# Routed experts of a mixture ranked on the chip by their number of tiles, and their weights loaded and split by rank along the loop, four instead of seven ahead of it

## The chip, the cores and the metric

One core of a Trainium2 chip runs the whole program. The metric is the device time of one execution in microseconds. Its engines are TensorE (PE; its weight loads are PEld), VectorE (DVE), ScalarE (ACT), GpSimd (POOL), and SyncE (SP), which here only issues DMAs.

## The reference, cut to what matters

The network has two layers on 2048 tokens of width 512. The change lies in the second half of the first layer, a mixture of experts: 2 shared experts that all tokens use, and 16 routed experts of which each token uses 4.

```python
flat = u.reshape(-1, d)                                  # 2048 x 512, layer norm of x
h = jax.nn.relu(jnp.einsum('td,ndf->ntf', flat, shared_w1) + shared_b1[:, None, :])
out = flat + jnp.einsum('ntf,nfd->td', h, shared_w2) + shared_b2.sum(0)
scores = jax.nn.sigmoid(flat @ centroids.T) + bias
vals, idx = jax.lax.top_k(scores, KR)                    # KR = 4 of NR = 16 experts
gating = jnp.zeros_like(scores).at[jnp.arange(T)[:, None], idx].set(vals)
gating = gating / jnp.clip(gating.sum(-1, keepdims=True), 1e-08)
# for each expert: rout += (relu(flat @ w1 + b1) @ w2 + b2) * g[:, None];  w1 512x352, w2 352x512
x = x + jnp.tanh(g_ffn[0]) * (out + rout)
```

## The kernel before

`phase_ffn` holds three stages; the attention and the second feed-forward part of layer 2 follow in `phase_back` and are untouched.

**Shared stage.** 16 blocks of 128 tokens go through a pipeline in 24 beats (`beats`): per block a norm on DVE, the two shared experts on PE (`up`: 72 matmuls of 128 columns, `down`: 18 of 512), the routing (`route`, `choose`, `count`, `place`) and four indirect DMAs from POOL (`scatter`) that write each (token, gate) pair into its expert's list in DRAM. DVE writes the result of a block in `finish`, SP stores it in `store`; `finish` of block n waits until the store of block n-2 has landed. While this runs, SP loads the first routed experts (`early`), ACT rounds them to the high f16 part (`split`, L1124) and DVE makes the low part (`low`, L1257), each in two halves. Before, these are 7 experts (`EARLY = 7`), one in every second beat from 5 on, both halves in one beat.

**Table.** When all lists are known, DVE computes in `table` how many tiles of 128 tokens each expert has (at least one) and which expert and which list row each of the N2 = 79 tiles uses. `numbers` turns the result into a row by two small matmuls, and DVE writes it as integers to `tab2`. SP's `lists_done` waits for it and for the lists, and loads the entries of tiles 0 to 3 (L991).

**Routed loop.** 79 tiles, in the order of the experts 0 to 15, whatever their sizes. A tile: SP loads its 128 entries (`entry_load`, L991), POOL gathers 128 rows of x (`roxg`, L1070), PE transposes them (L279; the output's name alternates between ps_shpR and ps_shpC), DVE copies them to SBUF (`evacuate`, L1311), PE does 36 matmuls with w1 (`rup`, L1444), ACT the relu (`rhidden`), ACT and DVE the high and low part, PE 9 matmuls with w2 (`rdown`, L1433), ACT scales by the gate (`rout`), POOL adds the rows to DRAM (L1077). PE works in beats: transposes of tile b, `rdown` of tile b-3, `rup` of tile b-1. Only the entries of tiles 0 to 11 are loaded without a condition; from 12 on SP loads those of tile b when the gather of tile b-2 has landed (`entries`), and the gather of a tile also waits for PE's transposes two tiles before. Both engines run in their program's order, so what SP waits for in between delays later entries.

The worst case is one tile for every expert, so expert n must be ready at tile n. Experts 7 to 13 are loaded right after the shared stage, expert 14 after the split of 13, the last in eight pieces; the splits are in these beats, and PE waits by itself:

```python
late_beat = {n: beat for n, beat in zip(range(EARLY, direct), (3, 4, 5, 7, 8, 9, 10, 12))}
small_beats = (12, 13, 14, 15)
...
e.wait_ge(S.sem("rolo"), 2 * (direct - 1))      # SP, last_weights, ahead of entry loads that follow
...
pipeline(e, N2, [..., (ready, 1, 0, direct), (small_ready, 1, direct, NR), ...], unroll=8)    # PE
```

`pipeline` writes a beat out as plain code where the set of its stages changes, and makes a hardware loop of `unroll` beats where at least two such rounds have the same set. PE's loop covers tiles 18 to 73 before (7 rounds of 8). The query weights of the next phase (1024 KB) are loaded in the loop at beat 42 (`query_weights`, L1037).

Of the kernel before, what the change touches and what calls it, by code (L numbers as in the profile page):

```python
# [175 lines left out]
def build(nc, a, out):  # L176
    with ExitStack() as ctx:
# [8 lines left out]
        def dram(name, shape, dt=f32):  # L186
# [23 lines left out]
            "tab2": sb(ctx, "tab2", [1, 2, N2], i32),  # L210
# [239 lines left out]
class Front:  # L450
# [68 lines left out]
    def sync(self, e):  # L519
# [18 lines left out]
        e.dma_start(small["part"][:, :], a["c_part"]).then_inc(S.sem("sh_part"), 16)  # L538
        for n in range(KEY_FIRST):
            keys.store_values(e, n)  # L540
# [302 lines left out]
PIECES = 4  # L843

# [13 lines left out]
def phase_ffn(nc, S, sb, ps, a, R, K, shared, routed, wt_at):  # L858
# [10 lines left out]
    EARLY, FIRST = 7, 12  # L869
    direct = NR - 1  # L870
    QW, QBEAT = KD * D, 42
    with ExitStack() as mem:
# [10 lines left out]
        part = sb(mem, "shpart", [P, 1])  # L883
# [9 lines left out]
        first_slots = wt_at + (NR - EARLY - 2) * 2 * EW  # L893
        near, far = Place(nc, nc.sbuf_base, first_slots), Place(nc, first_slots, nc.sbuf_top)
        front = Front(nc, S, a, R, K, shared, {"b1r": b1r, "bias": bias, "rb1": rb1, "part": part, "vt": vt, "sq": ksq, "ss": kss, "rr": krr}, far, near, pH, pY, pR)
# [23 lines left out]
        cnt, limit, tiles, skip, past = (sb(mem, "sh" + n, [P, NR]) for n in ("cnt", "limit", "tiles", "skip", "past"))  # L919
        sums = [sb(mem, f"shsums{i}", [P, NR]) for i in range(2)]  # L920
        more = sb(mem, "shmore", [P, NR, NR])
        which = sb(mem, "shwhich", [P, 2])
        tabf = sb(mem, "shtabf", [P, 2], f16)
# [17 lines left out]

        q_at, q_raw = final(0), final(1) // 2
# [15 lines left out]
        def _(e):  # L958
# [15 lines left out]

            def weights(n):
                at = raw_at(n)
                if n == 0:
                    S.wait(e, "kyv", turn_of(NT - 1))
                if n == EARLY - 2:
                    for p in range(2):  # L980
                        S.wait_moved(e, "kykout", turn_of(NT - 1 - p))
                e.dma_start(raw[:, at:at + W1], a["rw1"][n]).then_inc(S.sem(f"roraw{n}"), 16)
                e.dma_start(raw[:, at + W1:at + W1 + W2], a["rw2"][n]).then_inc(S.sem(f"roraw{n}"), 16)
# [18 lines left out]
            def lists_done(it):  # L1002
# [3 lines left out]
                e.wait_ge(S.sem("shtable"), 2)  # L1006
                first_entries(0, 4)

# [14 lines left out]
            def last_weights(it):  # L1023
                e.wait_ge(S.sem("rolo"), 2 * (direct - 1))
                weights(direct - 1)

            def small(it):
                for i in range(2):
                    j = (it.n - small_beats[0]) * 2 + i
# [3 lines left out]
                    e.dma_start(piece[j % 2][:, 0:cols], a[src][direct][:, at:at + cols]).then_inc(S.sem(f"ropiece{j % 2}"), 16)  # L1033
# [4 lines left out]
            pipeline(e, N2, [(entries, 0, FIRST, N2), (query_weights, 0, QBEAT, QBEAT + 1), (last_weights, 2, late_beat[direct - 2], late_beat[direct - 2] + 1),  # L1038
                             (small, 2, small_beats[0], small_beats[1]), (small, 2, small_beats[1], small_beats[-1] + 1)])

        @blk.gpsimd
        def _(e):
# [19 lines left out]
            for n in range(N2 + 5):  # L1062
# [10 lines left out]
                if n >= 5:  # L1073
                    it = It((n - 5) // 2, (n - 5) % 2)
                    S.wait(e, "roy", it)
# [7 lines left out]
        def _(e):  # L1083
# [34 lines left out]
            def split(n):  # L1118
                e.wait_ge(S.sem(f"roraw{n}"), 32)
                if n >= 2:  # L1120
                    e.wait_ge(S.sem("rolo"), 2 * (n - 1))
# [1345 lines left out]
```

## Time and profile before

| what | value |
|---|---|
| time, median of 3 runs | 1187.44 us (1183.65 to 1187.78) |
| profiled execution, first to last instruction (span) | 1172.7 us |
| its own time, what lies around the span included | not recorded for it alone; the three runs lie 11.0 to 15.1 us above the span |
| busy share of the span | PE 84%, DVE 60%, ACT 57%, POOL 43% |
| TensorE's mean granted clock | 0.946 |
| bytes moved | 170.87 MB, mean 146 GB/s; the highest of 40 slices 370 GB/s |
| one expert's weights | a DMA of 704 KB and one of 768 KB |
| shared stage on PE | 243.4 to 398.0 us |
| routed loop on PE | 398.0 to about 780 us |

The busy share is a mean over stages with different limits; a stage is read by the waits of PE in it. A timeline row gives start, duration, engine, line, operation, output<-inputs and, in brackets, how long the engine was idle before it and what ended that. SPq rows are the DMA issues of SP.

### The profile page before, as it was taken

How to read it: one execution, taken by the hardware profiler on the slowest of the kernel's cores; microseconds unless marked ns; L12 is line 12 of the kernel's file. 1: busy time of each engine (PE TensorE's matmuls, PEld its weight loads, DVE VectorE, ACT ScalarE, POOL GpSimd, SP SyncE). 2: the span in 40 equal slices, each digit the busy share in tenths (PEclk: the TensorE clock that was granted, in tenths of full speed). 3: DMA queues.
4: the chain of work that ended last, by engine and by line, in shares of the span. 5: the costliest groups of instructions: out<-in, count | busy, mean ns of one | idle time of the engine just before them, and what ended most of it. 6: DMA issues, size and time to landing. Idle time of an engine off the chain costs nothing. (4 is left out here: it accounts for less than half of the span.)

```text
span 1172.7 us, 27955 instructions
## 1 busy us (share of the span) xinstructions
PE 990.9 (84%) x9515; PEld 567.5 (48%) x9516; DVE 705.2 (60%) x1724; ACT 672.1 (57%) x1091; POOL 504.0 (43%) x442
## 2 busy tenths in 40 slices
PE   5888989968999978899999999955899888888740
PEld 2545556445677656677777777742122211111120
DVE  8676755578888457322223222216688787877687
ACT  4655545445544267444445444435777789899950
POOL 0222232156676265555556555532233343433422
PEclk9999999998999989999999999987899999999975
DMA  6534231389985496766666666648598687497211
GB/s 234 178 127 138 82 129 62 130 194 229 227 209 138 132 370 155 148 122 112 120 146 117 116 117 117 119 68 219 134 178 172 154 187 145 102 180 147 65 42 64
DMA packets 183494, 170.87 MB, mean 146 GB/s; under 512 B 137173, under 2 KB 138773, under 8 KB 182485
## 3 DMA queue, kind: packets, MB, share of 16 engines
q1 hardware_dynamic: 155554, 111.62, 36.9%
q0 software_dynamic: 25888, 56.43, 24.1%
q10 hardware_dynamic: 1954, 1.54, 0.4%
q8 instruction: 60, 0.98, 0.4%
q14 instruction: 38, 0.30, 0.1%
HBM read 80.82 MB, written 65.20 MB: 125 GB/s over the span
## 5 line engine op out<-in xcount | busy, mean ns | idle before, releaser
L2020 ACT ACTIVATE sb_atp<-ps_atpS 128x1024 f32<-128x1024 f32 x256 | 242.6, 1037 | 40.5 <-PE ps_atpS L1759 40.5
L1444 PEld LDWEIGHTS ps_shpH<-sb_roxT,sb_rowt 128*128 (+1 forms) x2844 | 170.3, 107 | 20.7 <-DVE sb_roxT L1311 1.8
L1444 PE MATMUL ps_shpH<-sb_roxT,sb_rowt 128*128 128x128 f16 (+1 forms) x2844 | 174.7, 221 | 1.6 <-DVE sb_roxT L1311 1.6
L1433 PE MATMUL ps_shpY<-sb_rowt,sb_rohhl 128*128 (+1 forms) x711 | 170.4, 386 | 3.3 <-DVE sb_rowt L1324 2.9
L1771 PE MATMUL ps_atpO<-sb_atp,sb_atv 128*17 128x512 f32 x1024 | 137.3, 609 | 34.0 <-ACT sb_atp L2020 28.7
L1167 ACT ACTIVATE sb_roh<-ps_shpH,sb_rob 128x128 f32<-128x128 f32 (+1 forms) x237 | 68.8, 361 | 103.5 <-PE ps_shpH L1444 100.6
L1070 POOL DMA_INDIRECT sb_roxg<-xn,sb_roentry x79 | 85.1, 1077 | 87.9 <-DMA sb_roentry<-list 62.0
L1433 PEld LDWEIGHTS ps_shpY<-sb_rowt,sb_rohhl 128*128 128x128 f16 (+1 forms) x711 | 67.4, 99 | 71.6 <-issue 7.8
L1156 ACT ACTIVATE sb_roy<-ps_shpY,sb_roentry 128x512 f32<-128x512 f32 x79 | 54.2, 686 | 78.6 <-PE ps_shpY L1433 75.0
L1058 POOL DMA_INDIRECT list<-sb_shentry,sb_shposb x64 | 74.0, 1157 | 33.5 <-DVE sb_shposb L1239 18.5
L1077 POOL DMA_INDIRECT x2a<-sb_roy,sb_roentry x40 | 65.5, 1637 | 44.2 <-ACT sb_roy L1156 41.8
L1311 DVE COPY sb_roxT<-ps_shpR 128x1024 f16<-128x1024 f16 x40 | 27.6, 690 | 94.0 <-PE ps_shpR L279 94.0
L1077 POOL DMA_INDIRECT x<-sb_roy,sb_roentry x39 | 62.1, 1593 | 49.5 <-ACT sb_roy L1156 48.2
L1759 PE MATMUL ps_atpS<-sb_atq,sb_atk 64*128 64x512 f16 x512 | 79.9, 392 | 1.4 <-DMA sb_atq<-qst 0.6
L1311 DVE COPY sb_roxT<-ps_shpC 128x1024 f16<-128x1024 f16 x39 | 26.9, 690 | 84.7 <-PE ps_shpC L279 84.7
L1316 DVE TENSOR_TENSOR sb_rohhl<-sb_roh,sb_rohhl 128x384 f16<-128x384 f32 x79 | 44.2, 560 | 41.8 <-ACT sb_rohhl L1172 41.7
L1369 PEld LDWEIGHTS ps_shpH<-sb_shxT,sb_shw 128*128 128x128 f16 (+1 forms) x1152 | 67.5, 108 | 3.3
L1369 PE MATMUL ps_shpH<-sb_shxT,sb_shw 128*128 128x128 f16 (+1 forms) x1152 | 68.6, 222 | 0.0
L1379 PE MATMUL ps_shpY<-sb_shw,sb_shhh 128*128 128x512 f16 (+1 forms) x192 | 61.7, 405 | 7.2 <-DVE sb_shhl L1244 7.2
L1771 PEld LDWEIGHTS ps_atpO<-sb_atp,sb_atv 128*17 128x17 f32 x1024 | 17.2, 96 | 94.9 <-ACT sb_atp L2020 86.0
L820 PE MATMUL ps_shpY<-sb_ctx,sb_l1hh 128*128 (+1 forms) x152 | 46.8, 390 | 18.2 <-issue 13.8
L810 PE MATMUL ps_shpH<-sb_l1xT,sb_ctx 128*128 128x128 f16 x912 | 60.1, 223 | 0.8 <-issue 0.7
(355 smaller groups left out, 1771.5 us busy)
## 6 DMA issues: line engine op xcount, KB each, us to landing
sb_rowt<-rw SPq DMA_DIRECT2D x15, 768.0 KB, 9.6
sb_rowt<-rw SPq DMA_DIRECT2D x15, 704.0 KB, 6.5
kst<-sb_kykp SPq DMA_DIRECT2D x16, 512.0 KB, 3.5
qst<-sb_quqp SPq DMA_DIRECT2D x12, 512.0 KB, 4.0
vst<-sb_kyvt SPq DMA_DIRECT2D x16, 272.0 KB
sb_atv<-vst SPq DMA_DIRECT2D x32, 136.0 KB, 3.9
sb_stage<-ctxT SPq DMA_DIRECT2D x4, 1024.0 KB, 7.4
sb_shxin<-x SPq DMA_DIRECT2D x16, 256.0 KB, 5.4
```

Source lines behind the costliest of these rows:

```text
L810: last = e.matmul(self.pP[n % 2][:, f * P:(f + 1) * P], w[:, bass.ds(ex * W + (k * D + f * P), P)], self.xT[n % 2][:, x0 + k, :], start=j ...
L1058: S.moved(e.indirect_dma_start(out=R["list2"], out_offset=bass.IndirectOffsetOnAxis(ap=posb[it.p][:, k:k + 1], axis=0), in_=entry[:, it.n, ...
L1070: S.moved(e.indirect_dma_start(out=xg[it.p][:, :], out_offset=None, in_=R["xn2"], in_offset=bass.IndirectOffsetOnAxis(ap=rentry[:, n, 0:1] ...
L1077: S.moved(e.indirect_dma_start(out=R["x1" if it.p else "x2a"], out_offset=bass.IndirectOffsetOnAxis(ap=rentry[:, n - 5, 0:1], axis=0), in_ ...
L1167: last = e.activation(rh[0:n, f * P:(f + 1) * P], rpH[it.p][0:n, f * P:(f + 1) * P], ACT.Relu, bias=rb1[0:n, bass.ds(ex["bias"] * FB + f, ...
L1369: last = e.matmul(pH[it.p][s][0:n, f * P:(f + 1) * P], w[:, o:o + n], x[:, k, :], start=j == 0, stop=j == len(terms) - 1)
L1379: last = e.matmul(pY[it.p][:, :], x[0:n, s, k * P:(k + 1) * P], w[0:n, s * W2 + k * D:s * W2 + (k + 1) * D], start=j == 0, stop=j == len(t ...
L1433: last = e.matmul(pY[it.p][:, :], hhl[it.p][0:n, x, k * P:(k + 1) * P], weight(value, 2 * W1 + w + k * D, n, D), start=j == 0, stop=j == l ...
L1444: last = e.matmul(rpH[it.p][0:n, f * P:(f + 1) * P], weight(ex["up"], w + k * FF + f * P, P, n), rxT[it.p][:, x + k, :], start=j % (3 * KD ...
L1759: last = e.matmul(pS[n % 3][:, s * SEQ:(s + 1) * SEQ], k[at][r, j, m * P:(m + 1) * P], q[at][r, j, :], start=True, stop=True)
L1771: last = e.matmul(pO[it.p][32 * i:32 * i + n, :], vv[it.n % 3][:, m, i * n:(i + 1) * n], pr[(it.n * 8 + 2 * m + i // 2) % 6][:, (i % 2) * ...
L2020: S.done(e.activation(pr[n % 6][:, :], pS[n % 3][:, :], ACT.Exp, scale=HD ** -0.5 / SA ** 2), "atexp")
```

## The change

Experts 0 to 3 keep ranks 0 to 3. The 12 others get a rank by their number of tiles, most tiles first, computed in `table` with all-pairs comparisons. Tiles run in the order of rank; with the large ones first, rank r cannot come before tile 4 + ceil(60 (r-4)/12), so ranks 4, 5, ... 15 are needed at tiles 4, 9, 14, ... 59. SP reads the row offset of the expert of a rank from `order` into a register and loads by that address. Splits run four tiles ahead, one half in each of two beats; the early ones come every third beat. A third row of `tab2` gives the expert for the bias. PE does not wait for the splits by itself any more: DVE waits for its own (`low_done`) before it hands on a tile.

```diff
+EARLY = 4
+def needed_at(rank):
+    return rank if rank < EARLY else EARLY + -(-(NT * KR - EARLY) * (rank - EARLY) // (NR - EARLY))
...
-        early_beat = {5 + 2 * k: k for k in range(EARLY)}
-        late_beat = {n: beat for n, beat in zip(range(EARLY, direct), (3, 4, 5, 7, 8, 9, 10, 12))}
-        small_beats = (12, 13, 14, 15)
+        early_beat = {5 + 3 * k: k for k in range(EARLY)}
+        split_at = {n: needed_at(n) - 4 for n in range(EARLY + 1, direct)}
+        split_at[EARLY], split_at[direct - 2], split_at[direct - 1] = 1, 43, 49
+        load_at = {n: split_at[n] - 2 for n in range(EARLY + 3, direct - 1)}
+        load_at[direct - 1] = split_at[direct - 1] - 1
+        small_at = (51, 53, 55, 57)
+        small_load = (51, 54, 56, 58)
...
+            def expert_rows(n):
+                if n < EARLY:
+                    return slice(n * P, (n + 1) * P)
+                return bass.ds(e.value_load(K["order"][0:1, n:n + 1], min_val=0, max_val=(NR - 1) * P), P)
...
+                if n > EARLY:
+                    e.wait_ge(S.sem("rolo"), 2 * (n if n == direct - 1 else n - 1))
+                rows = expert_rows(n)
+                e.dma_start(raw[:, at:at + W1], a["rw1"][rows, :]).then_inc(S.sem(landed(n)[0]), 16)
...
-                e.wait_ge(S.sem("shtable"), 2)
+                e.wait_ge(S.sem("shtable"), 3)
                 first_entries(0, 4)
+                e.wait_ge(S.sem("shorder"), 1)
+                weights(EARLY)
+                first_entries(4, 8)
...
-            for n in range(EARLY, direct - 1):
-                weights(n)
-                first_entries(min(2 * (n - EARLY) + 4, FIRST), min(2 * (n - EARLY) + 6, FIRST))
...
+            weights(EARLY + 1)
+            first_entries(8, FIRST)
+            weights(EARLY + 2)
...
-            pipeline(e, N2, [(entries, 0, FIRST, N2), (query_weights, 0, QBEAT, QBEAT + 1), (last_weights, 2, late_beat[direct - 2], late_beat[direct - 2] + 1),
+            pipeline(e, N2, [(entries, 0, FIRST, N2), (query_weights, 0, QBEAT, QBEAT + 1)] + [late(n) for n in load_at]
+                     + [(small, 0, beat, beat + 1) for beat in small_load])
...
-            def split(n):
-                e.wait_ge(S.sem(f"roraw{n}"), 32)
+            def split(n, half):
+                if half == 0:
+                    e.wait_ge(S.sem(landed(n)[0]), landed(n)[1])
...
+                tail(v.tensor_tensor(sortkey[:, :], tiles[:, :], mul, ALU.mult))
+                tail(v.tensor_tensor(sortkey[:, :], sortkey[:, :], add, ALU.add))
+                tail(v.tensor_tensor(before[:, :, :], cols(sortkey), rows(sortkey), ALU.is_ge))
+                tail.go(v.tensor_reduce(place_[:, :], before[:, :, :], AX.X, ALU.add))
...
+                    S.done(v.tensor_reduce(K["order"][0:1, :], more[0:1, :, :], AX.X, ALU.add), "shorder")
...
-                for i in range(2):
+                for i in range(3):
                     last = e.matmul(pCw[0:1, 2 * NR + i * N2:2 * NR + (i + 1) * N2], tabf[:, i:i + 1], K["ident"][:, 0:N2], start=True, stop=True)
...
-            pipeline(e, N2, [(ahead, 0, 1, N2 + 3), (turn, 0), (ready, 1, 0, direct), (small_ready, 1, direct, NR), (both, 1, 0, N2 + 2), (rup, 1)], unroll=8)
+            e.wait_ge(S.sem("rolo"), 2 * EARLY)
+            pipeline(e, N2, [(ahead, 0, 1, N2 + 3), (turn, 0), (both, 1, 0, N2 + 2), (rup, 1)], unroll=8)
```

SP issues the store of block 13 in the same beat as `lists_done` and after it. With the changed stage list PE's loop covers tiles 4 to 75 (9 rounds of 8). `QBEAT` goes from 42 to 44. POOL waits for the last stores of the shared stage before its first addition of rows.

## Rows read from the trace of the kernel before

**Rows 1.** Windows: stretch, us, busy PE, PEld, DVE, ACT, POOL, granted clock, DMA share, GB/s.
```profile
240.00:312.00 72.00, 56.03 (x641) 39.65 (x639) 63.45 (x178) 36.66 (x74) 43.75 (x40) 0.88 0.91 212
312.00:398.00 86.00, 86.00 (x1035) 62.27 (x1033) 66.42 (x212) 39.43 (x93) 56.92 (x53) 1.00 0.65 155
496.30:767.20 270.90, 265.97 (x3180) 200.88 (x3181) 76.72 (x121) 126.66 (x301) 153.91 (x120) 1.00 0.66 120
```

**Rows 2.** Timeline, TensorE in the early shared stage.
```profile
285.85 1.03 PE L1379 MATMUL ps_shpY<-sb_shw,sb_shhh 128*128 128x512 f16 x2 [2.99 <-DVE sb_shhl L1244]
```

**Rows 3.** The two lines that split routed weights: ns min/median/max, first and last start.
```profile
L1257 DVE SCALAR_TENSOR_TENSOR sb_rowt<-sb_rowt x30: 1619/1688/1754, 256.9 to 466.0; 128x1408 f16<-128x1408 f32 x15, 128x1536 f16<-128x1536 f32 x15
...
L1124 ACT ACTIVATE sb_rowt<-sb_rowt x30: 1364/1422/1475, 253.2 to 464.3; 128x1408 f16<-128x1408 f32 x15, 128x1536 f16<-128x1536 f32 x15
```

**Rows 4.** Timeline, TensorE from tile 0's up product to tile 18.
```profile
401.55 3.76 PE L1444 MATMUL ps_shpH<-sb_roxT,sb_rowt 128*128 128x128 f16 x36 [1.59 <-DVE sb_roxT L1311]
...
407.66 0.61 PE L279 MATMUL ps_shpC<-sb_ident,sb_roxg 128*128 128x128 f16 x8
...
417.07 1.04 PE L279 MATMUL ps_shpR<-sb_ident,sb_roxg 128*128 128x128 f16 x8 [4.85 <-DMA sb_roxg<-xn,sb_roentry]
...
424.05 0.61 PE L279 MATMUL ps_shpC<-sb_ident,sb_roxg 128*128 128x128 f16 x8
...
456.94 0.61 PE L279 MATMUL ps_shpR<-sb_ident,sb_roxg 128*128 128x128 f16 x8
...
485.90 2.76 PE L1433 MATMUL ps_shpY<-sb_rowt,sb_rohhl 128*128 x9 [2.88 <-DVE sb_rowt L1324]
...
496.31 0.61 PE L279 MATMUL ps_shpR<-sb_ident,sb_roxg 128*128 128x128 f16 x8 [0.24 <-issue]
```

**Rows 5.** Timelines, SP's queue and VectorE, at the handover and at tile 13.
```profile
391.80 3.76 SPq L991 DMA_DIRECT2D sb_roentry<-list  x4
...
395.60 5.64 SPq L967 DMA_DIRECT2D x2a<-sb_shxo  x3
...
456.28 0.33 SPq L982 DMA_DIRECT2D sb_rowt<-rw  x1
...
457.98 1.56 SPq L991 DMA_DIRECT2D sb_roentry<-list  x2
...
383.79 0.42 DVE L1271 TENSOR_REDUCE sb_shtiles<-sb_shmore 128x16 f32<-128x256 f32 x1
...
399.63 0.48 DVE L1249 TENSOR_SCALAR sb_shxs<-sb_shxs,sb_gate 128x512 f32<-128x512 f32 x1 [3.82 <-DMA x2a<-sb_shxo]
```

**Rows 6.** Timelines, TensorE and POOL: loop turn, plain tile, query load, last tile.
```profile
563.32 0.61 PE L279 MATMUL ps_shpC<-sb_ident,sb_roxg 128*128 128x128 f16 x8
...
568.53 0.61 PE L279 MATMUL ps_shpR<-sb_ident,sb_roxg 128*128 128x128 f16 x8 [0.65 <-issue]
...
577.41 0.61 PE L279 MATMUL ps_shpR<-sb_ident,sb_roxg 128*128 128x128 f16 x8
...
581.81 0.61 PE L279 MATMUL ps_shpC<-sb_ident,sb_roxg 128*128 128x128 f16 x8
...
600.38 0.62 PE L279 MATMUL ps_shpC<-sb_ident,sb_roxg 128*128 128x128 f16 x8 [0.79 <-DMA sb_roxg<-xn,sb_roentry]
...
614.81 0.61 PE L279 MATMUL ps_shpR<-sb_ident,sb_roxg 128*128 128x128 f16 x8
...
767.21 0.61 PE L279 MATMUL ps_shpR<-sb_ident,sb_roxg 128*128 128x128 f16 x8
...
587.82 0.98 POOL L1070 DMA_INDIRECT sb_roxg<-xn,sb_roentry  x1 [0.67 <-DMA sb_roentry<-list]
```

**Rows 7.** Landings: gathers undisturbed, gathers under weight loads, entry loads under them.
```profile
DMA to landing us min/median/max: 3.4/4.1/4.8
...
DMA to landing us min/median/max: 3.2/6.8/8.3
...
DMA to landing us min/median/max: 4.7/7.5/10.8
```

More of the change, by code:

```diff
@@ L918, in phase_ffn @@
         gr = sb(mem, "shgr", [P, 1])
[L919 to L923, printed above, removed]
+        cnt, tiles, sortkey, place_, sums, past = (sb(mem, "sh" + n, [P, NR]) for n in ("cnt", "tiles", "sortkey", "place", "sums", "past"))
+        more, before = (sb(mem, "sh" + n, [P, NR, NR]) for n in ("more", "before"))
+        which = sb(mem, "shwhich", [P, 3])
+        tabf = sb(mem, "shtabf", [P, 3], f16)
         assert nc.sbuf_base <= first_slots
@@ L1267, in table @@
                 tail.start(It(0, 0))
+                limit, mul, add, past_last, row, place1 = (rankc[:, i, :] for i in range(6))
+                rows = lambda z: bcast(z[:, 0:1], [(1, NR), (0, NR)])
+                cols = lambda z: bcast(z[:, 0:1], [(0, NR), (1, NR)])
                 tail(v.scalar_tensor_tensor(cnt[:, :], K["iota"][:, :], -float(CAP), base[NT % 2][:, :], ALU.mult, ALU.add))
-                tail(v.tensor_scalar(limit[:, :], K["iota"][:, :], float(P), None, ALU.mult))
-                tail(v.tensor_tensor(more[:, :, :], bcast(cnt[:, 0:1], [(1, NR), (0, NR)]), bcast(limit[:, 0:1], [(0, NR), (1, NR)]), ALU.is_gt))
+                tail(v.tensor_tensor(more[:, :, :], rows(cnt), cols(limit), ALU.is_gt))
@@ new lines, in table @@
+                tail(v.tensor_tensor(sortkey[:, :], sortkey[:, :], add, ALU.add))
+                tail(v.tensor_tensor(before[:, :, :], cols(sortkey), rows(sortkey), ALU.is_ge))
+                tail.go(v.tensor_reduce(place_[:, :], before[:, :, :], AX.X, ALU.add))
+                tail(v.tensor_tensor(more[:, :, :], before[:, :, :], cols(tiles), ALU.mult))
+                tail(v.tensor_reduce(sums[:, :], more[:, :, :], AX.X, ALU.add))
+                tail(v.tensor_scalar(past[:, :], sums[:, :], part[:, 0:1], None, ALU.is_le))
@@ new lines, in table @@
+                tail.go(v.tensor_tensor(cnt[:, :], past[:, :], tiles[:, :], ALU.mult))
+                tail(v.tensor_reduce(which[:, 0:1], past[:, :], AX.X, ALU.add))
+                tail.go(v.tensor_scalar(sums[:, :], place_[:, :], 1.0, which[:, 0:1], ALU.subtract, ALU.is_equal))
+                tail(v.tensor_reduce(which[:, 1:2], cnt[:, :], AX.X, ALU.add))
+                tail.go(v.tensor_tensor(which[:, 1:2], which[:, 1:2], part[:, 1:2], ALU.subtract))
+                tail(v.tensor_tensor(sums[:, :], sums[:, :], past_last, ALU.mult))
@@ L1289, in numbers @@
+                tail(v.tensor_tensor(more[0:1, :, :], cols(place_[0:1, :]), rows(place1[0:1, :]), ALU.is_equal))
+                tail(v.tensor_tensor(more[0:1, :, :], more[0:1, :, :], cols(row[0:1, :]), ALU.mult))
+                with nc.allow_low_precision(reason="one whole number"):
+                    S.done(v.tensor_reduce(K["order"][0:1, :], more[0:1, :, :], AX.X, ALU.add), "shorder")
             def numbers(it):
                 v.wait_ge(S.sem("shrow"), 1)
-                S.done(v.tensor_copy(K["tab2"][0:1, 0, :], pCw[0:1, 2 * NR:2 * NR + N2]), "shtable")
```

138 lines of the change are left out of this document (73 added, 65 removed).

## The prediction

> **What bounds the kernel now.** I first read the windows of the stages, then TensorE's timeline for the places where it waits, then who is late there. The reader is to see three different limits [rows 1]. In the early shared stage (240 to 312 us) VectorE is busy 63.5 of 72 us and TensorE only 56.0, at a granted clock of 0.88; TensorE waits for VectorE there, as in the row with 2.99 us, one of three such waits [rows 2]. From 312 us to the end of the stage TensorE is busy for the whole 86 us, so nothing that leaves VectorE's queue there can be won. In the routed loop from tile 18 TensorE is again the limit, 266 of 271 us. A plain tile takes 4.40 us (577.41 to 581.81) [rows 6]. Between tile 0 and tile 18 it isn't: that is where the kernel loses time. Tile 3 to 4 takes 9.41 us, 4 to 5 6.98, 5 to 12 together 32.89 against 7 x 4.40 = 30.8, and 12 to 18 39.37 against 26.4, a loss of 13.0 [rows 4]. The waits behind these have names. TensorE waits 4.85 us for the gather of tile 4 and 2.88 us for a piece of the last expert, and again for a gather at tile 13. There the reason is SP: it holds the load of expert 14 back until 456.28, and the entries of the next tiles are issued behind it, at 457.98 [rows 5]. After a 4.85 us wait the eight transposes take 1.04 us instead of 0.61, so the clock has gone to its lower level, 1.2 GHz, and a part of the loss is that [rows 4].
>
> **Part A, the shared stage.** A split costs VectorE two instructions of 1.69 us and ScalarE two of 1.42 [rows 3]. Three of seven leave the stage. Of those before tile-beat 10, where VectorE limits, experts 0, 1 and 2 become experts 0 and 1: 3.4 us less on VectorE, and one half instead of two in a beat. Against it, the load of expert 1 now stands in SP's queue directly ahead of a block's input, which VectorE needs next. A wait of TensorE also costs clock, 0.88 on the mean of this stretch. The bounds are 0 (the late input eats it) and 9 us (all three waits, 2 to 3 us each, with half as much again of lower clock). I take 2.5, near the 3.4 of VectorE. The other experts leave at no gain, as TensorE covers them; without that cover they would be worth 3.4 us each.
>
> **Part B, the handover, up to tile 12.** The table has 21 instructions before and 23 after, three for `order` among them; eight instead of two have 256 elements, and one of these takes 0.42 us [rows 5]. Six more are 2.5 us at most, less what smaller ones leave: 2 us. TensorE's `up` of the last block covers them, and the numbers are needed only with the landed lists at 391.8. If that cover is gone, they cost 2 us.
> What matters is SP's order. Four entry loads take 3.76 us; two weight issues and the next read of a number 1.70, up to 457.98 [rows 5]. Before, the store of block 13 is issued at 395.60. Now the load of expert 4 (1.4 with its register) and four more entry loads (3.8) come first: 400.8. VectorE waits for that store in its last `finish` but one step before it can copy tile 0: before, it was released at 399.63, 4.03 us after the issue, and the first `up` began at 401.55, 1.92 later. So this `up` begins at 400.8 + 4.0 + 1.9 = 406.7, 5.2 us later than now, behind a TensorE wait of nearly 7 us instead of 1.59. What is queued behind VectorE's wait is the copy of tiles 0 and 1, and all of PE's loop waits for these. The clock after the longer wait: 36 matmuls took 3.76 us after the 1.59 us wait, so half of that, 1.9, is the lower level; after the 4.85 us wait a tile took 6.98 instead of 4.40, 2.6 more. The difference, 0.7, is added.
> Then the order helps. Before, tile 4's entries were behind expert 7's load; now they are loaded before tile 0 is done. Tile 3 follows the first `up` by 6.1 us as now (401.55 to 407.66), tile 4 by 4.4 more: 406.7 + 6.1 + 0.7 + 4.4 = 417.9. With 0.5 for a gather beside the load of expert 5 it is 418.4, against 417.07. Tile 12 follows after 8 x 4.40 = 35.2 and 0.8 for the loads of experts 5 and 6 (seven loads cost 2.1 over the same tiles): 454.4 against 456.94, a gain of 2.5. The bounds are a gain of 6 (the store lands in 3 us and the clock recovers) and a loss of 3 (it lands behind expert 4, in 7 us, and the gather of tile 4 is late).
>
> **Part C, tiles 12 to 78.** Before: 767.21 - 456.94 = 310.3 us. After: 66 x 4.40 = 290.5. A turn of PE's hardware loop costs 0.89 us (563.32 to 577.41 less three tiles) [rows 6]; there are 8 after tile 11 instead of 6: 7.1. The query load costs 1.3: 581.81 to 614.81 are 33.0 us for seven tiles, less 30.8 and one turn; it stays. The small pieces are one every second beat and late by nothing that TensorE sees, 0.5 for their traffic.
> Open is the price p of each of the eight expert loads (ranks 7 to 14) that now lie in the steady loop. A half split beside a tile is covered: ScalarE is busy 126.7 of 270.9 us, some 2.1 of 4.40, and 1.42 more fits; VectorE has 1.2 and 1.69 fits. Without that cover two beats would cost up to 3 us. The load itself disturbs gathers. A gather in the plain loop is issued at 587.82 for the tile three after 581.81, at 595.0 [rows 6], and lands in 4.1 us [rows 7]: 3.1 us of slack. Under the seven loads a gather landed in 6.8 us at the median, which costs nothing, and in 8.3 at worst, which costs 1.1. The query load, 1024 KB against 1472, cost 1.3. So p lies between 0 and 1.3 x 1.44 = 1.9; I take 0.9, the middle, as no row decides: 7.2. The sum is 290.5 + 7.1 + 1.3 + 0.5 + 7.2 = 306.6, a gain of 3.7.
> TensorE's clock held through the query load: the 0.79 us wait is followed by transposes of 0.62 us [rows 6].
> The Trainium skill (TensorE: Matmul & The Clock Gate, Part 1) says that a TensorE that goes idle falls back to 1.2 GHz. If that held for waits of 0.8 us too, each load would cost 1.9 us more, the excess after the 1.59 us wait, 15 in all, and the sum below would come to 1194. The row speaks against it at this length.
>
> **The sum.** 2.5 + 2.5 + 3.7 = 8.7 us less. The span of the profiled execution would be 1164.0 instead of 1172.7; the median lies 14.7 above that span, and with the same distance it is 1179. After tile 78 nothing changes.
>
> **The rivals.**
> Same, within 0.5% (5.9 us; this is about what a measurement of this kernel can tell from no change): it would take A at 0 and p at 1.3 as the query load has it: 2.5 + 0.5 = 3.0 us less, 1184.4. For it speaks that the only load seen in the steady loop cost that; against it, that a gather under seven expert loads in a row still landed in 6.8 us at the median. Chance 0.33.
> Slower: the entry load of the next tile lands behind an expert's load, as under the seven loads (4.7 us at best, 10.8 at worst) [rows 7]. 10.8 is 6.1 late against the best, 3.1 of it slack, so p = 3.0 and C loses 24.0 instead of 7.2: 1179 + 16.8 = 1195.8. It decides from p = 2.0 on (no gain) and from 2.7 on (slower by 0.5%). Against it: the next entries are issued only when a gather has landed, 4.4 us or more after the load, when most of it is through. For it: a late gather takes its successor's entries with it. Chance 0.15.
> More than forecast: SP's loads hide wholly (p = 0) and TensorE's three early waits go: A 6, B 2.5, C 10.9, 1168. Chance 0.12.
> That the change doesn't do what it says I leave out: the order of loads, splits and tiles is written in the program, and 79 tiles are computed whatever the ranks.
>
> **How the numbers follow.** The forecast, faster by more than the 5.9 us and by less than "more", has 0.40, and "more" 0.12: faster by over 0.5% 0.52. Same 0.33, slower 0.15. The range goes from "more" (1168) past "same" with B at its bad end (3.0 less becomes 2.5 more, 1190) to 1192, which is p = 2.5 in the forecast; what is left out on both sides is some 0.2. The forecast's own range is 1173 to 1184 (p from 0.2 to 1.5).
>
> **What would show it.** A: the waits of TensorE for VectorE are shorter than 2.99 us, and the stage ends on TensorE 2.5 us before 398.0. B: the first store behind the entry loads at about 401, the first `up` of the loop at about 404 (A taken off), tile 4 with no wait of 5 us. C: 8 turns of 0.89, no wait at tiles 13 to 17, and at tiles 12, 17, 22, 27, 32, 37, 40, 47 waits of 0 to 1 us. I am wrong if these waits are over 2 us or come in pairs, if ScalarE waits for a weight landing, or if TensorE's wait ahead of the first `up` is far from 7 us.

## The result and the profile after

The kernel after takes 1181.61 us (median of 8 runs, 1179.49 to 1187.16), the kernel before, in 8 runs beside it, 1189.09 (1183.65 to 1194.88). The ratio is 0.9937, with a 95% interval of 0.9914 to 0.9961. The forecast was 1179 against 1187.44, a ratio of 0.9929.

The two profiled executions say the opposite. From the page of the profile after (the clock and the rate are lines of 40 slices):

```profile
span 1182.1 us, 27766 instructions
...
PE 990.5 (84%) x9516; PEld 566.6 (48%) x9517; DVE 707.1 (60%) x1727; ACT 671.1 (57%) x1091; POOL 504.7 (43%) x442
...
PEclk9989999979899989999999999987799989999975
...
GB/s 234 177 127 137 82 127 65 136 181 182 203 161 90 99 202 165 167 157 196 167 192 172 160 121 121 116 66 222 132 174 175 150 192 130 111 179 140 70 41 64
```

1182.1 us against 1172.7 would be 9.4 us slower. The execution shown of before was an exception: the span of a run lies 1.8 us under its time (1182.1 and 1183.89 us in the run whose trace is after's), not the 14.7 that the prediction put between that span and the median of before. With 1.8 us added, 1172.7 is 1174.5, below all eight times of before. So a second trace of each kernel was needed first. The stages are read by the starts of TensorE's transposes of tiles 0, 12 and 78, and by its first `up` of the shared stage (all in us; "behind" is from tile 78 to the end of the span):

| trace | first up | tile 0 | tile 12 | tile 78 | shared | 0 to 12 | 12 to 78 | behind |
|---|---|---|---|---|---|---|---|---|
| before | 243.4 | 398.0 | 456.9 | 767.2 | 154.6 | 58.9 | 310.3 | 405.5 |
| before, second trace | 243.4 | 404.8 | 468.4 | 779.0 | 161.4 | 63.6 | 310.6 | 405.3 |
| after | 243.9 | 407.6 | 464.5 | 773.9 | 163.7 | 56.9 | 309.4 | 408.2 |
| after, second | 244.1 | 398.2 | 455.9 | 766.6 | 154.2 | 57.7 | 310.7 | 409.9 |
| after, third | 242.7 | 389.3 | 447.4 | 758.9 | 146.6 | 58.1 | 311.5 | 407.2 |

The shared stage swings by 17 us between executions of one kernel. The first trace of after is 9.4 us longer, and 9.1 of them lie there; the other parts nearly cancel (0.5 before the first `up`, 2.9 less in the two parts of the loop, 2.7 more behind them). The two parts of the routed loop repeat within about 2 us (before, tiles 0 to 12, within 5), and they can be compared.

**The handover.** SP's queue and VectorE's row for the store of block 13, in the trace after; these answer to [rows 5]:

```profile
401.92 3.76 SPq L1021 DMA_DIRECT2D sb_roentry<-list  x4
406.67 0.26 SPq L1012 DMA_DIRECT2D sb_rowt<-rw  x1
407.12 0.34 SPq L1013 DMA_DIRECT2D sb_rowt<-rw  x1
408.22 3.71 SPq L1021 DMA_DIRECT2D sb_roentry<-list  x4
411.98 5.16 SPq L987 DMA_DIRECT2D x2a<-sb_shxo  x3
...
415.52 0.49 DVE L1286 TENSOR_SCALAR sb_shxs<-sb_shxs,sb_gate 128x512 f32<-128x512 f32 x1 [10.34 <-DMA x2a<-sb_shxo]
```

And TensorE, which answers to [rows 4]:

```profile
408.84 0.62 PE L280 MATMUL ps_shpC<-sb_ident,sb_roxg 128*128 128x128 f16 x8 [0.63 <-DMA sb_roxg<-xn,sb_roentry]
417.45 3.93 PE L1501 MATMUL ps_shpH<-sb_roxT,sb_rowt 128*128 128x128 f16 x36 [7.99 <-DVE sb_roxT L1361]
421.22 0.61 PE L280 MATMUL ps_shpR<-sb_ident,sb_roxg 128*128 128x128 f16 x8
...
428.56 0.61 PE L280 MATMUL ps_shpR<-sb_ident,sb_roxg 128*128 128x128 f16 x8 [0.32 <-DMA sb_roxg<-xn,sb_roentry]
```

The store goes out 10.06 us behind the first entry load instead of 3.80. VectorE idles 10.34 us for it, and TensorE 7.99 for VectorE. From tile 4 on (428.56, the last row) the 4.85 us wait of before is gone.

**The steady loop.** SP, TensorE and POOL around the load of one late expert. A plain tile is 4.40 us long, as in [rows 6]:

```profile
595.02 0.34 SPq L1012 DMA_DIRECT2D sb_rowt<-rw  x1
595.55 0.34 SPq L1013 DMA_DIRECT2D sb_rowt<-rw  x1
...
597.63 0.10 SPq L1021 DMA_DIRECT2D sb_roentry<-list  x1
...
605.29 0.11 SPq L1021 DMA_DIRECT2D sb_roentry<-list  x1
...
597.08 0.98 POOL L1103 DMA_INDIRECT sb_roxg<-xn,sb_roentry  x1 [1.92 <-DMA sb_roentry<-list]
...
604.76 0.98 POOL L1103 DMA_INDIRECT sb_roxg<-xn,sb_roentry  x1 [4.80 <-DMA sb_roentry<-list]
...
604.31 0.62 PE L280 MATMUL ps_shpC<-sb_ident,sb_roxg 128*128 128x128 f16 x8 [2.55 <-DMA sb_roxg<-xn,sb_roentry]
604.76 3.34 PE L1490 MATMUL ps_shpY<-sb_rowt,sb_rohhl 128*128 x9
607.90 2.65 PE L1501 MATMUL ps_shpH<-sb_roxT,sb_rowt 128*128 128x128 f16 x36
610.39 0.61 PE L280 MATMUL ps_shpR<-sb_ident,sb_roxg 128*128 128x128 f16 x8
```

The gather issued at 597.08 lands when TensorE goes on, at 604.3, after 7.2 us instead of 4.1 [rows 7]. The entries issued at 597.63 let the next gather start at 604.76, after 7.1 us. TensorE waits 2.55 us, and right behind the transposes its nine matmuls of `rdown` take 3.34 us instead of 2.11: the clock has fallen to 1.2 GHz, and this tile is 6.08 us long. In the window from 604.76 to 608.00 us the granted clock is 0.61 on the mean. The loss comes in a pair of tiles, 2.7 and 1.7 us, which the prediction named as a sign that it would be wrong.

### The profile page after: what moved, and what is told of

The parts are those of the page before. It is cut to its first block and busy times, and to the rows that moved or that the text cites. A ratio compares the mean times of both kernels' runs of the same rounds, so it can differ in the third digit from the quotient of the medians.

```text
span 1182.1 us, 27766 instructions
## 1 busy us (share of the span) xinstructions
PE 990.5 (84%) x9516; PEld 566.6 (48%) x9517; DVE 707.1 (60%) x1727; ACT 671.1 (57%) x1091; POOL 504.7 (43%) x442
## 5 line engine op out<-in xcount | busy, mean ns | idle before, releaser
L2073 ACT ACTIVATE sb_atp<-ps_atpS 128x1024 f32<-128x1024 f32 x256 | 242.7, 1035 | 43.4 <-PE ps_atpS L1812 43.1
L1490 PE MATMUL ps_shpY<-sb_rowt,sb_rohhl 128*128 (+1 forms) x711 | 167.7, 381 | 0.4 <-DVE sb_rohhl L1366 0.4
L1103 POOL DMA_INDIRECT sb_roxg<-xn,sb_roentry x79 | 79.8, 1010 | 121.4 <-DMA sb_roentry<-list 86.4
L1193 ACT ACTIVATE sb_roy<-ps_shpY,sb_roentry 128x512 f32<-128x512 f32 x79 | 54.1, 685 | 60.6 <-PE ps_shpY L1490 38.6
L1113 POOL DMA_INDIRECT x<-sb_roy,sb_roentry x39 | 65.1, 1670 | 30.3 <-ACT sb_roy L1193 24.6
L1426 PE MATMUL ps_shpH<-sb_shxT,sb_shw 128*128 128x128 f16 (+1 forms) x1152 | 71.2, 223 | 4.1 <-issue 3.9
L1293 DVE SCALAR_TENSOR_TENSOR sb_rowt<-sb_rowt 128x1408 f16<-128x1408 f32 (+1 forms) x30 | 50.7, 1690 | 36.4 <-ACT sb_rowt L1160 29.3
```

The source lines that it names most:

```text
L1103: S.moved(e.indirect_dma_start(out=xg[it.p][:, :], out_offset=None, in_=R["xn2"], in_offset=bass.IndirectOffsetOnAxis(ap=rentry[:, n, 0:1] ...
L1113: S.moved(e.indirect_dma_start(out=R["x1" if it.p else "x2a"], out_offset=bass.IndirectOffsetOnAxis(ap=rentry[:, n - 5, 0:1], axis=0), in_ ...
L1426: last = e.matmul(pH[it.p][s][0:n, f * P:(f + 1) * P], w[:, o:o + n], x[:, k, :], start=j == 0, stop=j == len(terms) - 1)
L1490: last = e.matmul(pY[it.p][:, :], hhl[it.p][0:n, x, k * P:(k + 1) * P], weight(value, 2 * W1 + w + k * D, n, D), start=j == 0, stop=j == l ...
L2073: S.done(e.activation(pr[n % 6][:, :], pS[n % 3][:, :], ACT.Exp, scale=HD ** -0.5 / SA ** 2), "atexp")
```

## The experiments

All ratios are against the kernel before, timed beside the kernel on the same chip. Where two kernels are compared that were not timed beside each other, only their ratios to before are. The two kernels themselves were run again for a second trace.

**c_before** (unchanged):

> The kernel before, unchanged, profiled once more. The first profile of before has a span of 1172.7 us, 11 us below the fastest of its timed runs, and the one of after 1182.1, in line with its timed runs. Theory 1 (the first profile of before was an unusually good execution): this span is 1182 to 1190, and the surplus lies in the shared stage, where TensorE then ends later than 398.0 us; the routed loop from tile 0 to tile 78 again takes 369 us. Theory 2 (the profile is representative and the change really costs 9.6 us in the shared stage, won back somewhere outside the span): span 1171 to 1175 and the shared stage ends at 398 again.

**c_after** (unchanged):

> The changed kernel, unchanged, timed beside before on the same chip as the experiments of this call. Ratio 0.991 to 0.997. Theory 1 (the shared stage varies from execution to execution by several us, in both kernels): its end on TensorE is anywhere from 398 to 410 us, the loop from tile 0 to tile 78 takes 366 us again within 2. Theory 2 (the change makes the shared stage 9 us longer): it ends at 406 to 409 again.

Before took 1186.18 us in the one run. After took 1179.74, ratio 0.9949 [0.9922, 0.9976]. Theory 1 of both runs held for the shared stage: the second trace of before ends it at 404.8 us, the second of after at 398.2. The loop from tile 0 to 78 took 374.2 us where before was expected to repeat 369, and 368.4 where after was expected at 366 within 2. In the second trace of before the wait of tile 4 for its gather is 10.81 us instead of 4.85, so what the new order of entries removes can be larger than the rows showed:

```profile
428.35 1.03 PE L279 MATMUL ps_shpR<-sb_ident,sb_roxg 128*128 128x128 f16 x8 [10.81 <-DMA sb_roxg<-xn,sb_roentry]
```

**e_store.** The handover alone: SP's stages in one beat are put in another order, the store first.

```diff
-beats([(lists_done, NT + 4, 0, 1), (load, 0, 0, NT), (store, 7, 0, NT), (turn, 2, 0, NT), ...
+beats([(load, 0, 0, NT), (store, 7, 0, NT), (lists_done, NT + 4, 0, 1), (turn, 2, 0, NT), ...
```

> The changed kernel with the store of block 13 issued by SP ahead of lists_done instead of behind the eight entry loads and expert 4. Theory of the prediction (part B: TensorE's 8.0 us wait before the first up product comes from this store alone): the wait falls to under 2 us, tile 2 comes 6 to 8 us earlier relative to tile 0, tile 78 too if no gather takes the place: ratio to before 0.985 to 0.990. Rival: the gather of tile 2 or 4, or the load of expert 4 that its split waits for, is late next, and takes most of it back: ratio 0.990 to 0.994, with a wait of 4 us or more for one of these.

Ratio 0.9918 [0.9892, 0.9943], median 1173.58, against 0.9949 of after, timed beside it. The theory's 0.985 to 0.990 was missed; the ratio is in the rival's range, with a wait for the gather of tile 2 of 2.79 us and not 4. Tiles 0 to 12 take 52.6 us instead of 57.7. The first `up` hardly waits; TensorE now waits for the gather of tile 2:

```profile
403.83 2.18 PE L1501 MATMUL ps_shpH<-sb_roxT,sb_rowt 128*128 128x128 f16 x36 [0.19 <-DVE sb_roxT L1361]
408.80 0.62 PE L280 MATMUL ps_shpR<-sb_ident,sb_roxg 128*128 128x128 f16 x8 [2.79 <-DMA sb_roxg<-xn,sb_roentry]
409.49 3.53 PE L1501 MATMUL ps_shpH<-sb_roxT,sb_rowt 128*128 128x128 f16 x36
```

So the store behind the entry loads costs 5 us of the loop, net of the 2.79 that take its place. The intervals of the two ratios overlap; the row of the wait carries this verdict, the times only agree with it.

**e_entries.** The order of the entries alone, in the kernel before: all entries of tiles 4 to 11 go ahead of the loads of experts 7 to 13.

```diff
-            for n in range(EARLY, direct - 1):
-                weights(n)
-                first_entries(min(2 * (n - EARLY) + 4, FIRST), min(2 * (n - EARLY) + 6, FIRST))
+            first_entries(4, FIRST)
+            for n in range(EARLY, direct - 1):
+                weights(n)
```

> The kernel before with one part of the change alone: the entries of tiles 4 to 11 are issued ahead of the loads of experts 7 to 13 instead of between them. Ranks, splits and early experts stay. TensorE waited 5.0 and 11.0 us at tile 4 in two profiles of before. Theory (these waits are entries queued behind expert loads): the wait at tile 4 is under 1 us and the ratio 0.992 to 0.997. Rival: the expert loads start some 7 us later, their splits are late, and the gathers beside them still wait: tile 12 comes no earlier, ratio 0.998 to 1.002.

Ratio 1.0052 [1.0032, 1.0072]: slower by 0.5%, outside the ranges of both the theory and the rival. TensorE's wait at tile 4 is gone, but SP, ScalarE and TensorE show where it went:

```profile
406.73 8.97 SPq L991 DMA_DIRECT2D sb_roentry<-list  x8
415.74 0.43 SPq L982 DMA_DIRECT2D sb_rowt<-rw  x1
...
424.53 2.75 ACT L1124 ACTIVATE sb_rowt<-sb_rowt 128x1408 f16<-128x1408 f32 x2 [12.47 <-DMA sb_rowt<-rw]
...
427.18 0.85 ACT L1167 ACTIVATE sb_roh<-ps_shpH,sb_rob 128x128 f32<-128x128 f32 x3
...
429.75 0.55 DVE L1316 TENSOR_TENSOR sb_rohhl<-sb_roh,sb_rohhl 128x384 f16<-128x384 f32 x1
...
430.49 3.53 PE L1433 MATMUL ps_shpY<-sb_rowt,sb_rohhl 128*128 x9 [12.29 <-issue]
```

Expert 7 now starts to load at 415.74, ScalarE waits 12.47 us for it with the split that stands ahead of its other work, and TensorE stands 12.29 us. The profile names no releaser for that wait, but the rows give the chain: the relu behind the split starts at 427.18, VectorE's low part of it ends at 430.30, and `rdown` starts at 430.49. In the kernel before, the early entries alone do not pay. That they pay in the kernel after because fewer experts are urgent there is the likely reading; no run has the ranks with the old order of entries.

**e_noload.** The steady loop without the eight loads: ranks 7 to 14 are not loaded, their splits read the split weights of rank 2, so that ScalarE and VectorE do the same number of instructions and the traffic is gone (from tile 12 to 78 ScalarE is busy 163.4 us and VectorE 114.1; in after 161.9 and 113.9).

```diff
-            pipeline(e, N2, [(entries, 0, FIRST, N2), (query_weights, 0, QBEAT, QBEAT + 1)] + [late(n) for n in load_at]
+            pipeline(e, N2, [(entries, 0, FIRST, N2), (query_weights, 0, QBEAT, QBEAT + 1)]
...
+                src, scale = (raw[:, at + x:at + x + cols], SW) if n < EARLY + 3 else (wt[:, final(2) + o:final(2) + o + cols], 1.0)
```

> The changed kernel without the loads of ranks 7 to 14: the splits stay in their beats but read the split weights of rank 2, so the experts of these ranks compute with other weights. Theory of the prediction (part C: each load costs TensorE p = 0.9 us): 7 us less than the changed kernel, ratio to before 0.987 to 0.989, no wait of TensorE for a gather between tiles 13 and 50 but one beside the query load. Rival 1 (the loads are hidden, the waits are of the tiles' own traffic): within 2 us of the changed kernel, 0.993. Rival 2 (p about 1.5 as the after profile's excess of 15 us over plain tiles suggests): 12 us less, 0.983.

**e_double.** Each of the eight loads is followed by a copy of the same bytes from DRAM to DRAM, extra work that nothing needs. The copies also write to DRAM, so the load beside the gathers is more than doubled.

```diff
+                if n >= EARLY + 3:
+                    e.dma_start(nc.dram_tensor(f"again1_{n}", (P, W1), f32).ap(), a["rw1"][rows, :]).then_inc(S.sem("again"), 16)
+                    e.dma_start(nc.dram_tensor(f"again2_{n}", (P, W2), f32).ap(), a["rw2"][rows, :]).then_inc(S.sem("again"), 16)
```

> The changed kernel with each of the eight loads followed at once by a copy of the same bytes to a DRAM buffer that nobody reads: the same traffic again, nothing else. Theory 1 (late beyond a slack): p more than doubles, to 4 or more (the second burst has no slack left), tiles 12 to 78 take 330 us or more, ratio over 1.01. Theory 2 (in proportion to traffic): p = 3.0, tiles 12 to 78 take 322 us, ratio about 1.004.

**e_halves.** The same bytes as after, in two bursts: the DMA of 704 KB goes one beat earlier than that of 768 KB.

```diff
-                return (lambda it: weights(n), 0, load_at[n], load_at[n] + 1)
+                return (lambda it: weights(n, part), 0, load_at[n] + part - 1, load_at[n] + part)
...
-            pipeline(e, N2, [(entries, 0, FIRST, N2), (query_weights, 0, QBEAT, QBEAT + 1)] + [late(n) for n in load_at]
+            pipeline(e, N2, [(entries, 0, FIRST, N2), (query_weights, 0, QBEAT, QBEAT + 1)] + [late(n, part) for n in load_at for part in range(2)]
```

> The changed kernel with each of the eight loads of ranks 7 to 14 issued in two parts: the 704 KB DMA one beat earlier, the 768 KB DMA in the old beat. Without these loads tiles 12 to 78 took 297.3 us on TensorE, with them 309.4 and 310.7, so a load costs 1.5 to 1.7. Theory 1 (a gather has 3.1 us of slack, and only the length of the burst beside it makes it late): half a burst stays inside the slack, p falls to 0 to 0.5, tiles 12 to 78 take 298 to 301 us, ratio to before 0.985 to 0.988. Theory 2 (the traffic as such costs, whatever its portions): p stays at 1.5, tiles 12 to 78 take 309 to 311 us, ratio 0.993 to 0.995.

| kernel | median us | ratio [95%] | tiles 12 to 78 | p, us for each of 8 loads |
|---|---|---|---|---|
| e_noload | 1164.44 | 0.9823 [0.9792, 0.9853] | 297.4 | 0 |
| e_halves | 1164.27 | 0.9821 [0.9783, 0.9859] | 299.1 | 0.2 |
| after, three traces | 1181.61 | 0.9937 [0.9914, 0.9961] | 309.4 to 311.5 | 1.5 to 1.8 |
| e_double | 1212.19 | 1.0213 [1.0171, 1.0254] | 346.3 | 6.1 |

p is the stretch less 297.4, divided by 8. On the mean of the eight loads it follows the size of one burst and not the bytes in all: with the same 11.5 MB it is 0.2 or 1.6, with a second burst behind each nearly 4 times as much. e_noload came out as its rival 2 said, e_halves and e_double as their theories 1, e_halves with a ratio still better than its 0.985 to 0.988. So there is a slack, and what counts is how far a delay reaches beyond it. Two views show it. Why POOL's gathers sat idle, from 456 to 640 us, and why the transposes of TensorE did, from 460 to 770 us (us, times), for before, after, e_noload, e_halves and e_double in turn (the last only in the second view):

```profile
  DMA sb_roentry<-list: 37.1, 26
...
  DMA sb_roentry<-list: 60.6, 30
...
  DMA sb_roentry<-list: 28.6, 28
...
  DMA sb_roentry<-list: 58.2, 36
```

```profile
  DMA sb_roxg<-xn,sb_roentry: 6.2, 3
...
  DMA sb_roxg<-xn,sb_roentry: 8.8, 8
...
  DMA sb_roxg<-xn,sb_roentry: 0.7, 1
...
  DMA sb_roxg<-xn,sb_roentry: 2.0, 2
...
  DMA sb_roxg<-xn,sb_roentry: 34.9, 11
```

In e_halves POOL waits for entries as long as in after, 58.2 us to 60.6. TensorE waits 2.0 us instead of 8.8 (11.1 and 11.8 in the other two traces of after), because few delays exceed the slack. The sum of POOL's idle time did not tell what TensorE lost; the size of the single wait did. That splits cost nothing holds as well: e_noload has all of them, and its loop shows only loop turns and the query load.

The slack itself is not fixed. Take a tile as due 4.40 us after the tile before it; how long before that its gather is issued is the gather's lead. From 485 to 640 us the median lead is 7.4 and 7.1 us in the two traces of before and 7.3 in e_noload, but 5.1 to 5.2 in the three of after and 5.5 in e_halves: gathers that wait for entries go out later, and the lead doesn't recover between the loads. How late a gather lands and what it costs are then two things, as the query load shows in before and in e_best (described below), where it is one whole burst of 1024 KB:

```profile
592.17 0.98 POOL L1070 DMA_INDIRECT sb_roxg<-xn,sb_roentry  x1 [0.62 <-DMA sb_roentry<-list]
...
588.51 0.98 POOL L1105 DMA_INDIRECT sb_roxg<-xn,sb_roentry  x1 [0.30 <-issue]
...
589.03 0.61 PE L280 MATMUL ps_shpR<-sb_ident,sb_roxg 128*128 128x128 f16 x8
```

In before the gather landed 8.2 us after its issue (600.38 [rows 6]) with a lead of 7.2, and TensorE waited 0.79 us. In e_best it landed 8.5 us after its issue (596.99) with a lead of 4.9 (589.03 + 4.40 - 588.51), and TensorE waited 3.38. In the second trace of before the query load cost nothing: the tiles beside it take 4.40 us, or the 5.21 and 4.49 of every loop turn there. This is read from rows; no run changed the lead alone.

The Trainium skill (DMA: Bandwidth & Descriptors, Queues, rings and completion order) says that a DMA engine consumes the descriptors of one ring in order and changes between the rings of different queues a packet at a time. The entry loads stand in SP's queue as the weights do, and the entries issued 2.1 us behind them took 7.1 us; this agrees. The gather is in another queue (POOL's) and took as long, 7.2 us; so in this one instance the ring's order is not the whole cause, and no run here put the entries into another queue to tell the two apart.

**e_early7 and e_early7b.** After, with the loads and splits of three more experts in the shared stage as before, one expert in every second beat and both halves in one beat (extra work: they are done again by rank). The same kernel was timed twice, the second time beside after (c_after2).

```diff
-        early_beat = {5 + 3 * k: k for k in range(EARLY)}
+        early_beat = {5 + 2 * k: k for k in range(7)}
...
-                    if it.n - half in early_beat:
-                        low(early_beat[it.n - half], half)
+                    if it.n in early_beat:
+                        n = early_beat[it.n]
+                        if n < EARLY:
+                            low(n, half)
...
```

> The changed kernel with the early loads and splits of before put back in the shared stage: experts 0 to 6, one in every second beat, both halves in one beat. The results for experts 4 to 6 are not used and the ranks 4 to 6 are loaded and split again as in the changed kernel, so only the shared stage differs. Part A of the prediction: three splits more cost the shared stage 2.5 us, ratio to before 0.996 to 0.998. Rival 1 (the stage's time on TensorE is set by other things, transposing DMAs above all, and swings by 5 us by itself): no difference from the changed kernel, 0.993 to 0.995. Rival 2 (the lower traffic and the single halves matter more than I put them): 5 us or more, ratio 0.998 to 1.000.

> The kernel with seven early experts in the shared stage again (experts 4 to 6 split there and once more by rank). It measured 0.9973 against 0.9937 and 0.9949 of the changed kernel, in other calls. If part A is right (2.5 us), this run is 0.1% to 0.4% above the changed kernel of this call. If the stage only swings by itself, it is within 0.1%.

> The changed kernel again, timed in the same rounds as the next run, so that part A is read from two kernels under the same conditions. Ratio to before 0.992 to 0.996. Its shared stage on TensorE took 163.7 and 154.2 us in two profiles, its loop 366.3 and 368.4; another value in these ranges is expected.

e_early7 was at 0.9973 [0.9947, 0.9998]. As e_early7b it was at 0.9972 [0.9953, 0.9991], and after, timed beside it, at 0.9953 [0.9933, 0.9972], medians 1177.05 and 1175.83 us. That is 1.2 us for part A by the medians and 2.2 by the ratios, in the forecast's direction, with overlapping intervals. The shared stages of all the traces say no more: 146.6 to 163.7 us, mean 156.2, in the nine traces with four early experts, and 154.6 to 163.3, mean 157.8, in the five with seven. The trace shows the mechanism plainly. With seven early experts the wait of [rows 2] is there, in e_early7b:

```profile
264.98 1.04 PE L1461 MATMUL ps_shpY<-sb_shw,sb_shhh 128*128 128x512 f16 x2 [3.17 <-DVE sb_shhl L1299]
```

In the three traces of after no wait of TensorE for VectorE of over 1 us stands between the stage's first `up` and tile 0. What stands there instead is a late DMA. After, the windows of the stretch of [rows 1], and SP, VectorE and TensorE at its end:

```profile
240.00:312.00 72.00, 56.82 (x665) 41.55 (x664) 56.71 (x176) 33.79 (x72) 47.82 (x43) 0.88 1.05 183
```

```profile
305.91 5.08 SPq L992 DMA_TRANSPOSE sb_shxT<-sb_shxhl  x1
...
312.97 0.44 SPq L983 DMA_DIRECT2D sb_shxin<-x  x1
...
316.79 0.70 DVE L1239 BATCH_NORM_STATS2 sb_shst<-sb_shxin 128x6 f32<-128x512 f32 x1 [7.48 <-DMA sb_shxin<-x]
...
318.79 0.49 PE L1404 MATMUL ps_shpR<-sb_shcen,sb_shxT 128*128 128x16 f16 x12 [3.97 <-DMA sb_shxT<-sb_shxhl]
```

VectorE is busy 6.7 us less than before (56.71 to 63.45) and TensorE nearly the same (56.82 to 56.03). In this execution SP needed 5.08 us to issue a transposing DMA that takes it 1.2 to 2.2 at the other places from 238 to 375 us, the block's input went out late at 312.97, and VectorE stood 7.48 us. In the third trace of after (shared stage 146.6 us) its longest such wait at this place is 0.80 us, and TensorE is busy 59.85 us of the 72, VectorE 64.69; so most of the 6.7 us is time in which VectorE stood, and not work that had left. The gain depends on the execution. The first trace has the end of part A's lower bound, 0 because "the late input eats it", but not its cause: the input that followed the load of expert 1 (267.26 us) made nobody wait, and what came late was the issue of a transposing DMA. Why that took 5.08 us stays open.

**e_best and e_best2.** Both changes together, the store first and the loads in two bursts. e_best2 also loads the query weights in two halves in two beats.

```diff
-            pipeline(e, N2, [(entries, 0, FIRST, N2), (query_weights, 0, QBEAT, QBEAT + 1)] + ...
+            pipeline(e, N2, [(entries, 0, FIRST, N2), (query_weights(0), 0, QBEAT - 1, QBEAT), (query_weights(1), 0, QBEAT, QBEAT + 1)] + ...
```

> The changed kernel with both: the store of block 13 ahead of the entry loads, and the loads in two parts in two beats. If the two gains add (0.3% from the store as measured, 0.6 to 0.9% from the halves by theory 1): ratio to before 0.982 to 0.985, and the loop from tile 0 to 78 takes 351 to 354 us on TensorE. If the halves give nothing (theory 2): 0.991 to 0.993 as the store alone, loop 362 us.

> The kernel with the early store and the loads in two parts, and the query load of 1024 KB too in two parts in two beats. In the profile of that kernel TensorE lost 3.6 and 2.2 us at tiles 43 and 44, one loop turn of 0.9 included, with the query load the only whole one left. By theory 1 of the halves these losses go to under 1 us beside the turn: 3 to 5 us less, ratio 0.975 to 0.979, the loop from tile 0 to 78 350 us or less. If the loss came from the last pieces of expert loads nearby, no difference: 0.979.

e_best: 1162.35 us, 0.9789 [0.975, 0.9829], tiles 0 to 12 in 50.2 us, 12 to 78 in 302.9. Of the 3.8 us that TensorE's transposes still wait for gathers, 3.38 are at the query load, and this wait drops the clock at once, to transposes of 1.04 us:

```profile
588.98 0.50 SPq L1072 DMA_DIRECT2D sb_rowt<-wqT  x1
...
596.99 1.04 PE L280 MATMUL ps_shpC<-sb_ident,sb_roxg 128*128 128x128 f16 x8 [3.38 <-DMA sb_roxg<-xn,sb_roentry]
```

e_best2: 1154.95 us against 1180.24 of before, 0.9771 [0.9742, 0.98]. This beats before by 2.3% and after, timed beside it at 1175.83, by 1.8%. It is not told apart from e_best. The one wait for a gather beside the query load is now 0.37 us, but the loop from tile 0 to 78 takes 354.4 us where 350 or less was expected and e_best took 353.1: 302.1 from tile 12 to 78, against 302.9 in e_best and 299.1 in e_halves. What the halved query load gives is not shown; two executions of kernels with the same whole query load, e_halves and e_best, differ by more.

## Why the prediction was right, and which terms were off

The total was right: faster, 5.5 to 7.5 us by the ratios of the three comparisons (0.9953, 0.9949, 0.9937; 4.4 to 7.5 by the medians) against 8.7. The parts were not of the forecast size, and that the sum came near is in part luck: the 3.7 us of part C are missing, and a part B above its forecast stands in for some of them.

**Part A** (forecast 2.5): 1.2 to 2.2 us by the paired times, not told apart from zero by intervals. The mechanism is shown: TensorE's waits for VectorE went, and came back in e_early7b. The size is not settled, since the stage moves by 17 us from one execution to the next.

**Part B** (forecast 2.5): tiles 0 to 12 take 57.6 us on the mean of three traces (56.9, 57.7, 58.1) against 61.3 of two (58.9, 63.6), 3.7 us less. Every link was there, near its size: the store 10.06 us behind the entries (9.0 forecast, from 391.8 to 400.8; the load of expert 4 with its register took 2.5 us, 405.68 to 408.22, and not 1.4), VectorE released 3.54 us behind it (4.0), the `up` 1.93 later (1.92), TensorE's wait 7.99 us ("nearly 7"), tile 4 with 0.32 us. The stretch after was forecast at 56.4 us (454.4 less 398.0) and is 1.2 longer. Of that, 0.7 is a turn of TensorE's hardware loop: the first of the 8 turns lies between tiles 11 and 12, and the prediction booked it in part C. The gain is larger than forecast only because of before, whose wait at tile 4 is 4.85 us in one trace and 10.81 in the other; against the first trace alone, which the forecast used, it is 1.3. The prediction also took half of the 3.76 us of the first `up` as the lower clock's share, 1.9; at full speed these 36 matmuls take 2.17 (421.66 us of the trace after), so the share is 1.6.

**Part C** (forecast 3.7): 310.5 us before, 310.5 after (means of 310.3 and 310.6, and of 309.4, 310.7 and 311.5). This term was wrong, and it gave nothing. The base was 2.0 us better than forecast (290.5 + 7.1 + 1.3 + 0.5 = 299.4, measured 297.4): there are 7 turns behind tile 12 and not 8, and one costs 0.78 us and not 0.89, which together is some 1.6. The step that failed is the sentence "p lies between 0 and 1.3 x 1.44 = 1.9; I take 0.9, the middle". Measured, p is 1.5 to 1.8, so the loads cost 12 to 14 us instead of 7.2. The upper bound was near; to halve it had no ground in the steady loop. Three things were wrong there. It took the cost of one query load in one trace as that load's price: the same 1024 KB cost 1.3 us there, nothing in the second trace of before and 5 in e_best. It took the 3.1 us of slack of a plain loop (a lead of 7.2 less a landing of 4.1) to hold behind loads too; between the loads the lead is 5.1 to 5.2 us, so the median landing of 6.8, which "costs nothing" in the prediction, would by this estimate cost 1.6. And it assumed, against the slower rival, that the next entries are issued "4.4 us or more after the load"; the row of 597.63 stands 2.1 us behind the load's second DMA, and these entries landed in 7.1 us. What the slower rival named, entries late behind an expert's load, was there; whether it set TensorE's wait is open, and p stayed under the 2.0 from which it would have taken the gain.

**The rivals.** "Same" put p at 1.3 and A at 0: nearer in its terms than the forecast (p 1.6, A 1 to 2), and its sum was 3.0 us less, where 5.5 to 7.5 were measured. "Slower" had p at 3.0. "More" needed p at 0, which e_halves almost reaches, with 1164.27 us against the rival's 1168.

**The absolute time.** It came out 2.6 us over the forecast. The way there had an error that cancelled: the sum was made on a span 11 us under the time of the fastest run beside it, and the 14.7 us from that span to the median of other runs were added again, where only 1.8 lie around a span.

**What is open.** Whether the late gather or the late entries set TensorE's wait at a load, as no run put one into another queue. And behind tile 78, where nothing changes, after's three traces take 407.2 to 409.9 us and before's two 405.3 and 405.5; the other kernels here with the ranks lie at 405.2 to 407.2, so it was not followed further. With it, the parts of the traces don't add up to the gain: the mean span of after's three is 1174.9 us, of before's two 1178.5, 3.6 less, with 3.0 lost behind tile 78 and with a shared stage that differs by more from trace to trace. The gain of the total rests on the timed runs alone.

## What to carry to other kernels

A large load that is spread into a steady pipeline isn't priced by its bytes but by how long one burst delays the small transfers that the pipeline hangs on, against their slack, and the loads before it have used up a part of that slack. Split it until each piece fits in; here that was worth more (14 to 16 us, by the ratios of e_halves and after) than the change that spread the loads (7 us). Don't issue small loads that a later stage needs ahead of a store that the next stage waits for, when both stand in one queue. And before a span is used as the base of a sum, set it beside the spans of the other runs: one trace of each kernel here gave a sign that was wrong.

## What was not expected

TensorE's clock survived longer waits than the 0.79 us of [rows 6]. After 2.17 us (tile at 541.07 us of the trace after) transposes and `rdown` ran at full speed, with 0.62 and 2.11 us. After 2.55 us the transposes did (0.62) and the matmuls behind them didn't (3.34). After 3.38 us (e_best) the transposes were slow already, 1.04 us. In the handover the matmuls were slow after 1.59 us [rows 4], where TensorE had done only 16 short transposes since the last block. The Trainium skill (TensorE: Matmul & The Clock Gate, Part 1) says that a TensorE that goes idle falls back to 1.2 GHz; the rows agree that it happens, and show that the length of the wait alone does not decide it: 2.17 us in the busy loop was survived, 1.59 behind sixteen short transposes was not.

```profile
541.07 0.62 PE L280 MATMUL ps_shpR<-sb_ident,sb_roxg 128*128 128x128 f16 x8 [2.17 <-DMA sb_roxg<-xn,sb_roentry]
541.52 2.11 PE L1490 MATMUL ps_shpY<-sb_rowt,sb_rohhl 128*128 x9
```
